# Self-attention's maxima: one 1024-column reduction per query tile, over two neighbouring banks

## The reference

```
sim  = einsum('bhid,bhjd->bhij', q, k) * scale      # 1024 x 1024 for each batch and head
attn = softmax(sim, axis=-1)                        # subtracts a value for each query row i, then exp
out  = einsum('bhij,bhjd->bhid', attn, v)
```

## Time and profile before

| | |
|---|---|
| median of 3 runs | 2253.82 us (2253.4 to 2254.86) |
| the profiled execution's own time | 2252.54 us |
| its span | 2250.8 us |
| busy PE (TensorE's matmuls) | 2140.9 us, 95% |
| busy DVE (VectorE) | 1678.2 us, 75% |
| busy ACT (ScalarE) | 1474.6 us, 66% |
| busy POOL (GpSimd) | 1271.4 us, 56% |

### The profile page before, as it was taken

How to read it: one execution, slowest core, us unless ns; L and a number is a source line. 1 busy time by engine, 2 the same in 40 slices (tenths; PEclk the granted TensorE clock), 3 DMA queues, 4 the chain that set the end, 5 groups by cost and what they waited for, 6 DMA issues and landing times.

```text
span 2250.8 us, 59613 instructions
## 1 busy us (share of the span) xinstructions
PE 2140.9 (95%) x25456; PEld 1438.4 (64%) x25456; DVE 1678.2 (75%) x3214; ACT 1474.6 (66%) x1948; POOL 1271.4 (56%) x794
## 2 busy tenths in 40 slices
PE   5999999999999999999999999998999999999899
PEld 2566666675666666667566666675746666667675
DVE  6888887567588888665768888866577888885564
ACT  3788889335388888833548888873354888886342
POOL 4678877223277877722327887762233887774231
PEclk8999999999999999999999999999999999999999
DMA  3222220010232232001032222100103223210000
GB/s 115 71 73 63 60 72 26 11 39 18 69 93 55 61 78 61 28 1 39 24 88 74 63 75 74 44 28 1 39 17 90 81 68 81 53 37 21 11 11 20
DMA packets 60216, 114.22 MB, mean 51 GB/s; under 512 B 9392, under 2 KB 21680, under 8 KB 59952
## 3 DMA queue, kind: packets, MB, share of 16 engines
q1 hardware_dynamic: 59952, 110.41, 18.0%
HBM read 55.72 MB, written 4.19 MB: 27 GB/s over the span
## 4 chain that ended last, share of the span: by engine, by line
PE 67%; DVE 20%; ACT 8%; issue 3%; POOL 1%; DMA 0%; DVEq 0%; SPq 0%; POOLq 0%; ACTq 0%
PE work L872 8%; DVE minima L1447 7%; PE scores L787 6%; PE scores L789 6%; PE scores L788 6%; PE scores L902 6%; PE scores L895 6%; PE work L787 4%; PE work L789 4%; PE work L788 4%; PE work L924 3%; PE work L920 3%; PE work L922 3%; DVE prob L1463 3%; ACT prob L1263 2%
## 5 line engine op out<-in xcount | busy, mean ns | idle before, releaser
L734 POOL TENSOR_TENSOR prob<-prob 128x1024 f16<-128x1024 f32 x320 | 682.6, 2147 | 366.9 <-ACT prob L1264 351.2
L1447 DVE TENSOR_REDUCE minima<-work 128x1 f32<-128x512 f32 x1024 | 683.2, 682 | 57.3 <-PE work L872 53.4
L1263 ACT ACTIVATE prob<-scores 128x1024 f32<-128x1024 f32 x512 | 525.6, 1027 | 99.6 <-PE scores L902 82.0
L1264 ACT ACTIVATE prob<-scores 128x1024 f16<-128x1024 f32 x512 | 523.4, 1022 | 0.0
L924 PE MATMUL work<-vals,prob 128*128 128x65 f16 x4096 | 429.5, 196 | 0.0
L922 PE MATMUL work<-vals,prob 128*128 128x64 f16 x4096 | 429.3, 193 | 0.0
L920 PE MATMUL work<-vals,prob 128*128 128x65 f16 x4096 | 428.8, 193 | 0.4
L920 PEld LDWEIGHTS work<-vals,prob 128*128 128x128 f16 x4096 | 382.8, 99 | 68.4 <-issue 19.0
L872 PE MATMUL work<-ka,qa 128*128 128x512 f16 x1024 | 389.7, 383 | 31.2 <-DVE minima L1447 19.1
L922 PEld LDWEIGHTS work<-vals,prob 128*128 128x128 f16 x4096 | 379.7, 97 | 54.1
L924 PEld LDWEIGHTS work<-vals,prob 128*128 128x128 f16 x4096 | 380.1, 97 | 0.0
(11 more groups left out here) (165 smaller groups left out, 4389.7 us busy)
## 6 DMA issues: line engine op xcount, KB each, us to landing
qa<-staged_q SPq DMA_DIRECT2D x128, 128.0 KB, 2.3
ka<-staged_k SPq DMA_DIRECT2D x128, 128.0 KB, 2.3
raw_even<-in_pairs SPq DMA_DIRECT2D x32, 384.0 KB, 3.3
raw_odd<-in_pairs SPq DMA_DIRECT2D x32, 384.0 KB, 3.3
raw_odd<-in_pieces SPq DMA_DIRECT2D x20, 512.0 KB, 3.4
raw_even<-in_pieces SPq DMA_DIRECT2D x20, 512.0 KB, 3.5
qb<-staged_q SPq DMA_DIRECT2D x64, 128.0 KB, 2.3
kb<-staged_k SPq DMA_DIRECT2D x64, 128.0 KB, 2.3
```

The lines of the kernel that those rows point to most:

```text
L734: pool.tensor_tensor(prob[1][:, slot, :], prob32[:, slot, :], prob[0][:, slot, :], ALU.subtract).then_inc(a.polished, 1)
L1263: act.activation(prob32[:, n % RING, :], source, ACT.Exp)
L1264: act.activation(prob[0][:, n % RING, :], source, ACT.Exp)\
L1447: dve.tensor_reduce(minima[:, t, h:h + 1], out[:, :], AX.X, ALU.max, negate=True)\
```

## The change

The two banks are now one tensor of 1024 columns, `peaks`. A tile has one "max" entry: its two matmuls go, one right after the other, into the two halves, and one reduction of 1024 columns reads both and writes the half-float column of `shift16`. `minima` and the "combine" step are gone. The ring has one place (`PEAK_RING` = 1), so a maximum or a shift waits until the one before it has been read. A shift uses the first half of the same tensor. In the list of a step, a tile's second matmul thereby moves from behind the score to ahead of the placed projections. In steps with two tiles the second tile comes behind the score's takes. Beside the feed-forward's projections a tile stands after chunks 0 and 4, instead of half a tile after chunks 0, 2, 4 and 6.

```diff
-SCORE_RING, PEAK_RING, HIGH_RING = 2, 2, 1
+SCORE_RING, PEAK_RING, HIGH_RING = 2, 1, 1
...
-    tiles = [[Step("max", (t, h), par, head, 0) for h in range(BLKS)] for t in range(TILES)]
+    tiles = [[Step("max", t, par, head, 0)] for t in range(TILES)]
...
-    for half in range(2):
-        last = (half + 1) * HALF - 1
-        tiles[last] = tiles[last] + [Step("combine", half, par, head, 0)]
...
         out += [step for step in peaks_of[s] if step.kind == "arrive"] + peaks[:1]
-
-        spread = [peaks[1:2], peaks[2:3], peaks[3:]] if len(peaks) > 2 else [[], peaks[1:], []]
-        ends = [step for step in peaks_of[s] if step.kind == "combine"]
-        out += placed[s] + spread[0]
+        out += placed[s]
         out.append(Step("score", s, par, head, 0))
         out += [take(step) for step in placed[s] if step.kind in HIGH]
-        out += spread[1] + ([] if spread[2] else ends)
+        out += peaks[1:]
...
-        if spread[2]:
-            out += spread[2] + ends
...
-        work = [ps(f"work{i}", BLK) for i in range(4)]
+        peaks = ps("peaks", 2 * BLK)
+        work = [peaks[:, 0:BLK], ps("work1", BLK), peaks[:, BLK:2 * BLK], ps("work3", BLK)]
...
-                    pe.wait_ge(a.peak_free, pace.n(*PEAK) + 1)
-                    return self_peaks[pace.here(*PEAK) % PEAK_RING]
+                    pe.wait_ge(a.peak_free, pace.n(*PEAK) + PEAK_RING)
...
-                        out = next_peak()
-                        t, h = s
-                        pe.matmul(out[:, :], qa[par][head][:, t * P:(t + 1) * P],
-                                  ka[par][head][:, h * BLK:(h + 1) * BLK], start=True, stop=True)\
-                            .then_inc(a.peak_full, 1)
+                        next_peak()
+                        for h in range(BLKS):
+                            last = pe.matmul(work[2 * h], qa[par][head][:, s * P:(s + 1) * P],
+                                             ka[par][head][:, h * BLK:(h + 1) * BLK], start=True, stop=True)
+                        last.then_inc(a.peak_full, 1)
...
-                        out = next_peak()
-                        pe.wait_ge(a.shift_combined, pace.n("shift") + 1)
-                        pe.transpose(out[0:SHIFT_W, 0:P // 2].bitcast(F16), shift16[s][:, :], ident16[:, :])\
+                        next_peak()
+                        pe.transpose(work[0][0:SHIFT_W, 0:P // 2].bitcast(F16), shift16[s][:, :], ident16[:, :])\
                           .then_inc(a.peak_full, 1)
...
-                        dve.tensor_reduce(minima[:, t, h:h + 1], out[:, :], AX.X, ALU.max, negate=True)\
-                           .then_inc(a.peak_free, 1)
-                    elif step.kind == "combine":
-                        dve.wait_ge(a.peak_free, pace.n(*PEAK) + PEAK_RING)
-                        dve.tensor_reduce(shift16[s][:, 0:HALF], minima[:, s * HALF:(s + 1) * HALF, :],
-                                          AX.X, ALU.min)\
-                           .then_inc(a.shift_combined, 1)
+                        next_peak()
+                        dve.tensor_reduce(shift16[s // HALF][:, s % HALF:s % HALF + 1], peaks[:, :], AX.X, ALU.max,
+                                          negate=True).then_inc(a.peak_free, 1)
```

More of the change, by code:

```diff
@@ L272, in self_steps @@
     for n, tile in enumerate(maxima(0, 0)[:HALF]):
-        at = 1 + max(i for i, step in enumerate(tile) if step.kind == "max" and step.step[1] == 0)
-        out += tile[:at] + [mark(f"max{n} first")] + tile[at:] + [mark(f"max{n}")]
+        out += tile + [mark(f"max{n}")]
     out += [Step("shift", 0, 0, 0, 0), mark("shift")]
@@ L363, in build @@
         scores = [ps(f"scores{i}", 2 * BLK) for i in range(2)]
-        work = [ps(f"work{i}", BLK) for i in range(4)]
+        peaks = ps("peaks", 2 * BLK)
+        work = [peaks[:, 0:BLK], ps("work1", BLK), peaks[:, BLK:2 * BLK], ps("work3", BLK)]
         four = [scores[i][:, h * BLK:(h + 1) * BLK] for i in range(2) for h in range(2)]
         self_outs = work[3]
-        self_peaks = [work[0], work[2]]
         self_high = work[1]
@@ L422, in build @@
         prob = [sb(f"prob{i}", [P, 4, TOKENS], F16) for i in range(2)]
-        minima = sb("minima", [P, TILES, 2])
         shift16 = [sb("shift16", [P, SHIFT_W], F16)]
@@ L480, in build @@
         names = ("peak_full peak_free work_full work_high work_free scores_full exp_done refined polished probs_used "
-                 "outs_free inverse_ready head0_ready head1_ready shift_combined row_ready")
+                 "outs_free inverse_ready head0_ready head1_ready  row_ready")
         a = collections.namedtuple("Sems", names)(*[sem(f"self_{n}") for n in names.split()])
@@ L866, in do @@
                     elif step.kind == "max":
-                        if head == 1 and s == (0, 0):
+                        if head == 1 and s == 0:
                             pe.wait_ge(a.head1_ready, pace.n("arrive", times=8 * MOVES) + CREDIT)
-                        out = next_peak()
-                        t, h = s
-                        pe.matmul(out[:, :], qa[par][head][:, t * P:(t + 1) * P],
-                                  ka[par][head][:, h * BLK:(h + 1) * BLK], start=True, stop=True)\
-                            .then_inc(a.peak_full, 1)
+                        next_peak()
[3 more added lines that the diff above has]
+                        last.then_inc(a.peak_full, 1)
                     elif step.kind == "shift":
-                        out = next_peak()
-                        pe.wait_ge(a.shift_combined, pace.n("shift") + 1)
-                        pe.transpose(out[0:SHIFT_W, 0:P // 2].bitcast(F16), shift16[s][:, :], ident16[:, :])\
+                        next_peak()
+                        pe.transpose(work[0][0:SHIFT_W, 0:P // 2].bitcast(F16), shift16[s][:, :], ident16[:, :])\
                           .then_inc(a.peak_full, 1)
@@ L1180, in feed_forward @@
                     if ahead and t in (4, 5):
-                        names = [f"max{2 * (t - 4) + i}{end}" for i in range(2) for end in (" first", "")]
-                        beside = {c: (lambda name=name: ahead(name)) for c, name in zip((0, 2, 4, 6), names)}
+                        names = [f"max{2 * (t - 4) + i}" for i in range(2)]
+                        beside = {c: (lambda name=name: ahead(name)) for c, name in zip((0, 4), names)}
                     project(index, t, 6, beside=beside)
@@ L1441, in do @@
                     elif step.kind == "max":
[L1442 to L1446, removed]
-                        dve.tensor_reduce(minima[:, t, h:h + 1], out[:, :], AX.X, ALU.max, negate=True)\
-                           .then_inc(a.peak_free, 1)
-                    elif step.kind == "combine":
-                        dve.wait_ge(a.peak_free, pace.n(*PEAK) + PEAK_RING)
-                        dve.tensor_reduce(shift16[s][:, 0:HALF], minima[:, s * HALF:(s + 1) * HALF, :],
-                                          AX.X, ALU.min)\
-                           .then_inc(a.shift_combined, 1)
+                        next_peak()
+                        dve.tensor_reduce(shift16[s // HALF][:, s % HALF:s % HALF + 1], peaks[:, :], AX.X, ALU.max,
+                                          negate=True).then_inc(a.peak_free, 1)
                     elif step.kind == "shift":
-                        out = next_peak()
+                        next_peak()
                         dve.wait_ge(a.row_ready, pace.n("shift", times=16) + CREDIT)
-                        dve.tensor_copy(shift_rows[:, :], out[0:HALF, 0:P // 2].bitcast(F16))\
+                        dve.tensor_copy(shift_rows[:, :], work[0][0:HALF, 0:P // 2].bitcast(F16))\
                            .then_inc(a.peak_free, 1)
```

## The result

The changed kernel takes 2353.08 us (2352.81 to 2354.26), the one before 2254.03 us beside it; the ratio is 1.0442, with a 95% interval of 1.043 to 1.0454. The change costs 99 us. The forecast was 2340 us, 86.5 more than before, in a range of 2285 to 2360. Two executions in this document's series, one of the kernel before and one of a variant, took 3640 and 3697 us at a mean granted clock of 0.557; no comparison here rests on them.

What follows compares the result with a forecast made beforehand. TensorE was taken as the bound, so its stalls lengthen the kernel; inner pairs +57.6, first pairs +18.8, last pairs +3.2 and the rest +6.9 sum to +86.5 us on 2253.8, giving 2340 us, range 2285 to 2360.

Steps and rivals of the forecast that it cites:

- The reduction: Wide maxima reduction on VectorE: 1.19 us for 1024 columns, saving 0.1 us a tile, costed at nothing except where TensorE waits.
- The shifts: Four places in an inner pair where the next maximum waits for VectorE's copy: +0.1, +0.3, +0.9, +1.1, together +2.4 us.
- the fourth: Head 1's step 4: copy waits behind the refine, +0.9, or +1.3 us if GpSimd stretches it; +1.1 taken.
- The other stages: Everything outside the inner pairs: first pairs +18.8, last pairs +3.2, feed-forward and first-round start together +6.9 us.
- openings: Tiles beside the feed-forward's projections, +1.2 us for each of 3 rounds, and the first round's four tiles, +3.3: +6.9 us.
- four first pairs: First pair of each round: first unit's two-tile steps +2.3, its head 1 +2.4, so +4.7 each, +18.8 us.
- 24 inner pairs: 6 inner pairs in each of 4 rounds, +2.4 us each from waits behind the shifts: +57.6 us.
- four last pairs, to the last shift: Last pair of each round, only head 0 has maxima behind its shifts: +0.8 each, +3.2 us.
- A: Rival, 12%: VectorE keeps ahead, refines end before the shift's transposition; 2287 us.
- B: Rival, 6%: the change is a gain, one instruction fewer per tile removes most of today's waits; about 2235 us.
- C: Rival, 5%: waits only change places, +0.8 us a pair at the shifts met by 0.8 less elsewhere; 2254 us.
- D: Rival, 4%: stalls near 1 us, four in a pair, make TensorE's granted clock drop; 2450 us.

Runs made afterwards that it cites:

- the run with two reads: Changed kernel, its order and one-place ring kept, but the 1024 columns read by two 512-column reductions with the combine of before: 2366.43 us, 1.0496 of before.

## Why the prediction was right

**What bounds the kernel.** TensorE did: an inner pair grew by 2.78 us, and by the matmuls' starts its stalls ahead of the maxima by 2.98 us (1.37 to 4.35); two small waits elsewhere went.

**The reduction** was priced at 1.19 us and took 1.22. The estimate from the Trainium skill's cycles (VectorE: DVE Perf Modes, section on the errata), 1.19 us, agrees with the trace within 0.04 us. I had costed what VectorE saves at nothing but for where it holds TensorE; the run with two reads puts it at 13 us, once the ring makes TensorE wait. VectorE's busy time fell by 21.7 us, not by the 74 and more that I named. Added up, its instructions' durations did fall by 77 us (the refines grew by 13.7), but before 151 us of them overlapped in the record, now 96, so some 55 of the 77 us had never been busy time of their own.

**The shifts.** Three of the four terms came out within 0.02 us, and the copy's waiting behind the refine is in the trace and was shown by cutting the refine short. The mis-sized term is the fourth, head 1's step 4: 1.1 was taken as the middle of 0.9 and 1.3, and it measured 1.37. The stretched refine was there in 23 of 24 inner pairs (mean stay 1.71 us), not in half of them. Over 24 pairs this and the 0.1 us beside it make 9 us.

**The other stages.** By the starts of the matmuls, to the last shift of the trace, with a pair running from the first maximum of its first unit (an opening is what lies before the first pair, from the start or from the last shift of the round before):

| stretch | forecast more, us | measured more, us |
|---|---|---|
| openings | 6.9 | 6.8 |
| four first pairs | 18.8 | 22.7 |
| 24 inner pairs | 57.6 | 67.6 |
| four last pairs, to the last shift | 3.2 | 2.5 |
| together | 86.5 | 99.7 |

The terms are rounded; the medians of the runs lie 99 us apart, 12.5 above the forecast.

Besides the inner pairs it is the first unit of a round that was priced too low: forecast 2.3 us, measured 4.4, 3.3, 3.3 and 2.6 in the four rounds. Part of this is a term that the sum put at nothing, the clock. The windows of the first unit before and after (second round), then of a stretch inside it, then of the fourth round's:

```profile
600.56:628.49 27.93, 23.54 (x218) 12.16 (x216) 23.16 (x43) 18.64 (x23) 10.00 (x5) 1.00 0.46 124
...
629.52:660.76 31.24, 24.97 (x219) 12.95 (x217) 22.79 (x27) 18.54 (x23) 11.22 (x5) 0.95 0.41 110
645.62:649.03 3.41, 3.08 (x29) 1.91 (x30) 1.44 (x2) 1.54 (x2) 0.00 (x0) 0.50 0.00 0
...
1786.03:1816.58 30.55, 23.69 (x219) 12.24 (x217) 22.79 (x27) 18.54 (x23) 11.22 (x5) 1.00 0.42 113
```

For 3.41 us the granted clock is 0.50, after three stalls of 1.3 to 1.4 us in the 16 us of the unit before it. It fell so in the first unit of the second and third rounds and for 6.8 us in that of the first, not in the fourth, whose first unit is 0.7 us shorter than the second's.

**The rivals.** A (VectorE keeps ahead) fell: the copies were late at both of head 1's shifts. B (a gain), to which the rule of the Trainium skill (VectorE: DVE Perf Modes, rules for kernel authors) on the count of operations would lead, fell too; 640 fewer instructions stand beside 99 us more. C fell: other waits did not shrink by what the shifts' grew. D, a clock that falls between the stalls of a pair, did not come true as priced: the clock of an inner pair's window is 1.00, with stalls of 1.5 us in it. But it was not wrong everywhere. The granted clock was at its lower level for 44.4 us of the changed kernel's span and for 20.5 before. In the traces of all seven kernels with a ring of one place it drops in the first unit of at least two rounds; in those of the five with two places it never does. By the second and fourth rounds, one drop of 3.4 us costs 0.7 us, so in the first units this is some 3 us of the 99, an estimate; what sets it off is not shown.

## What to carry to other kernels

Before two buffers of a ring are joined into one wide one, list every user of the ring, not only the one that is widened: here the small shift, with its copy 0.2 us long, took the only place, and the user right behind it paid for all that stood ahead of the copy on the other engine. Count a handover through a ring of one place as issue, latency, the queue ahead of the reader, and the reader. Where such a step is not urgent, give it a place in the order with some work of the waiting engine behind it; this alone took 16 us off the kernel before. The place matters: behind one more matmul the gain was gone (2259 us).

## What the runs showed of the hardware

VectorE's refine, with two float and half-float inputs in SBUF, has no fixed price. Alone it takes 1.22 us. Begun 0.19 us into a GpSimd instruction of 0.83 us it took 1.71, and begun 0.52 us into one of about 2.13 us it took 2.69: each time roughly what is left of GpSimd's instruction, plus its own 1.2. In the trace of the kernel before, the 98 refines that begin with no GpSimd instruction under way take 1.23 us at most, and the 94 others take what is left of GpSimd's instruction plus 1.07 to 1.18 us. In five of the kernels its mean was 1287, 1349, 1420, 1604 and 1652 ns, for the same work at other times. The Trainium skill (SBUF — State Buffer, section on SBUF's two separate sides) says that such an operation of VectorE and GpSimd take a shared pair of ports in turns for a whole instruction, whoever starts first; these lengths agree with that, though no run here isolates it. Three of my expectations, which moved refines or tiles, had a fixed price for the refine and missed; the longer refines are in the traces of all three.
